# A 16-sequence, four-layer kernel: output product with its operands exchanged, row factors spread by transfers, gates applied on ScalarE, new instruction orders

## The reference, cut to what matters

```python
# B, per head h of 8, expert e of 8; gm is the gate of the chosen expert, else 0
gm = one_hot(argmax(sigmoid(x @ w_gate))) * gates
values = einsum('bhne,ehdk,bnd->bhnk', gm, value_experts, x)
attn = softmax(causal(q * SCALE @ k.T))
out = einsum('bhij,bhjk->bhik', attn, values)
out = einsum('bhne,ehkd,bhnk->bhnd', gm, output_experts, out).sum(heads)
x = layernorm(x + out)
# C: rotation of q and k in pairs of features
rope(x) = stack([x1 * cos - x2 * sin, x2 * cos + x1 * sin])
```

## Time and profile before

| what | value |
|---|---|
| median of 3 runs | 1497.77 us (1497.28 to 1497.99) |
| the profiled execution | 1495.65 us, span of its instructions 1493.8 us |
| TensorE matmul, busy | 1434.7 us, 96% |
| VectorE, busy | 1205.2 us, 81% |
| ScalarE, busy | 820.6 us, 55% |
| GpSimd, busy | 748.6 us, 50% |
| `token_blocks` | from 0 to 1005 us |
| `soft_experts` | from 1005 us to the end |

### The profile page before, as it was taken

One profiled execution on the slowest core, in us unless ns is written; L12 is line 12 of the kernel. 1 busy time (PEld: TensorE's weight loads), 2 busy tenths in 40 slices (PEclk: granted clock), 3 DMA queues, 4 the chain that ended last, 5 costly groups with the idle time before them and its releaser, 6 DMA issues. The chain is left out here.

```text
span 1493.8 us, 32591 instructions
## 1 busy us (share of the span) xinstructions
PE 1434.7 (96%) x10940; PEld 1267.7 (85%) x10940; DVE 1205.2 (81%) x2359; ACT 820.6 (55%) x1850; POOL 748.6 (50%) x1833
## 2 busy tenths in 40 slices
PE   8789999999999999999999999988999999898998
PEld 6658888888888888888888887867999999898998
DVE  6778889889888898898898887768888888757664
ACT  4354555454555464455555544306776777667775
POOL 1433346346355354454453451226777777467772
PEclk8889999999999999999999999998999999999999
DMA  5100000000000000000000004007777777887872
GB/s 194 61 8 8 1 15 2 14 16 1 15 15 2 16 5 12 15 5 12 16 1 15 8 1 128 2 3 174 196 193 193 191 192 195 264 315 297 312 304 75
DMA packets 135426, 130.43 MB, mean 87 GB/s; under 512 B 7232, under 2 KB 125248, under 8 KB 128768
## 3 DMA queue, kind: packets, MB, share of 16 engines
q1 hardware_dynamic: 135296, 128.79, 27.9%
HBM read 72.93 MB, written 55.84 MB: 86 GB/s over the span
## 5 line engine op out<-in xcount | busy, mean ns | idle before, releaser
L737 PE MATMUL ps_l<-ve_f,oe 128*128 128x128 f32 x2048 | 275.7, 279 | 0.8 <-DVE ve_f L1740 0.8
L737 PEld LDWEIGHTS ps_l<-ve_f,oe 128*128 128x128 f32 x2048 | 248.8, 192 | 23.1 <-issue 20.4
L1740 DVE SCALAR_TENSOR_TENSOR ve_f<-ps_s,oT 128x512 f32<-128x512 f32 x248 | 166.7, 681 | 4.1 <-PE ps_l L737 2.3
L2934 POOL TENSOR_TENSOR d_s<-d_ex 128x1024 f32<-128x1024 f32 x31 | 125.2, 4040 | 83.0 <-ACT d_ex L2684 82.8
L1701 DVE COPY_PREDICATED vals<-oh,ps_l 128x1024 f32<-128x1024 int32 x112 | 146.9, 1312 | 19.3 <-PE ps_l L477 17.4
L2559 PE MATMUL ps_s<-d_ex,arena 128*128 128x128 f32 x1024 | 121.1, 277 | 4.6 <-DVE d_ex L2827 4.6
L2559 PEld LDWEIGHTS ps_s<-d_ex,arena 128*128 128x128 f32 x1024 | 118.2, 194 | 5.0 <-DVE d_ex L2827 5.0
L2547 PE MATMUL ps_l<-arena 128*128 (+1 forms) x960 | 114.5, 279 | 3.9 <-ACT d_raw L2679 3.9
L1293 ACT ACTIVATE ve_f<-ps_l,r 128x128 f32<-128x128 f32 x128 | 47.3, 370 | 125.9 <-DVE r L1713 125.6
L2547 PEld LDWEIGHTS ps_l<-arena 128*128 128x128 f32 x960 | 111.9, 195 | 4.1 <-ACT d_raw L2679 4.1
L475 PE MATMUL ps_l<-veH,x1H 128*128 128x512 f32 x256 | 115.2, 450 | 0.1
(11 more groups left out here) (332 smaller groups left out, 3842.7 us busy)
## 6 DMA issues: line engine op xcount, KB each, us to landing
logits<-d_raw SPq DMA_DIRECT2D x128, 256.0 KB, 3.5
e_lt<-logits SPq DMA_DIRECT2D x32, 1024.0 KB, 5.1
y_slots<-d_ys SPq DMA_DIRECT2D x64, 256.0 KB, 4.6
d_ex<-y_slots SPq DMA_DIRECT2D x8, 1024.0 KB, 6.9
e_y<-y_slots SPq DMA_DIRECT2D x6, 1024.0 KB, 7.2
d_w<-W SPq DMA_DIRECT2D x16, 256.0 KB, 3.4
arena<-xT SPq DMA_DIRECT2D x16, 128.0 KB, 2.4
arena<-x SPq DMA_DIRECT2D x16, 128.0 KB, 2.4
```

Source lines behind the costliest of these rows:

```text
L737: last = pe.matmul(ps_u[:, cols], oe[:, hp, e, :], mo[:, n % MO, hp, :], start=False, stop=(e == NE - 1 and hp == HP - 1), skip_group_chec ...
L1740: V.scalar_tensor_tensor(mo[:, n % MO, :, :].rearrange("p a n -> p (a n)"), chosen_of(b, c), float(NE - e), oT[:, u, c, :, :].rearrange("p ...
L2934: G.tensor_tensor(s8[:], part[:, 0:8, :], part[:, 8:16, :], ALU.add).then_inc(n, 1)
```

## The change

1. **Output product.** `b_out` has `mo` as stationary and `oe` as moving operand. The sum comes out with tokens in the partitions, in `ps_m` instead of the second half of `ps_l`. `b_oa` and `b_oat` are gone; `b_res` reads the sum itself. `b_start`, which puts the residual there, has four matmuls of 128 columns instead of two of 256.
2. **Factors by transfers.** `b_rgs`, `b_rgb`, `b_oht`, `b_choice` and the four `b_ot` multiplications are gone. VectorE writes the 16 factors and 16 numbers of each token into `rn`; TensorE turns them once (`b_rnt`, 32x128), ScalarE copies them (`b_rn`), and SP writes 16 KB to DRAM and reads them back into all partitions (`spread`, two transfers of 512 KB into `nb`). ScalarE copies the attention's output (`b_ot`, 2 x 512 columns), one VectorE multiplication of 1024 columns applies the factors (`b_og`), and `b_mo` compares with the numbers in SBUF.
3. **Gate of the values.** `b_vg` is gone; `b_pt` applies the gate as a scale of each row of the turned probabilities, in two activations of 256 and 128 columns instead of one copy of 384.
4. **Scores in two groups.** `b_scores(g)` and `b_pv(g)` take two pairs of heads at once, in both pairs of PSUM banks; `b_rg` runs once.
5. **Rotation.** For the blocks below 13 the pairs are swapped by two transfers from SBUF to SBUF (`swap`); `c_rot` is left for the last three.
6. **Orders.** The orders in `slot`, in the first blocks and in the tail are new on all five engines. `newton`, which computes the roots, is the same in both kernels.

The diff, cut to its core:

```diff
+            def spread(b):
+                sp.wait_ge(q["b_rn"], b + 1)
+                wait(sp, q["b_nb"], 32 * (b - 1))
+                sp.dma_start(rn_dram[b % 2].rearrange("a r n -> (a r) n"), rows_s[0:4 * C * HP, :]
+                             ).then_inc(q["b_rn_out"], 16)
+                sp.wait_ge(q["b_rn_out"], 16 * (b + 1))
+                wait(sp, q["b_mo"], OUTS * b)
+                for a in range(2):
+                    sp.dma_start(nb[DH * a:DH * (a + 1), :, :, :, :].rearrange("p q c h n -> p (q c h n)"),
+                                 rn_dram[b % 2, a:a + 1].rearrange("a r n -> a (r n)").to_broadcast([DH, 2 * C * HP * P])
+                                 ).then_inc(q["b_nb"], 16)
+            def swap(b):
+                sp.wait_ge(q["c_q"], b + 1)
+                wait(sp, q["c_qr"], 2 * b)
+                sp.dma_start(t1[0:P:2, :, :], ql[1:P:2, :, :]).then_inc(q["c_swap"], 16)
+                sp.dma_start(t1[1:P:2, :, :], ql[0:P:2, :, :]).then_inc(q["c_swap"], 16)
...
             for pair in range(2, NB // 2 - 1):
                 for u in range(2):
+                    spread(2 * pair + u - 2)
                     load(2 * pair + u + 1, 1 - u)
+                    swap(2 * pair + u - 3)
                     store(2 * pair + u - 3)
...
+            def b_rnt(b):
+                pe.wait_ge(q["b_rg"], 2 * (b + 1))
+                wait(pe, q["c_x3t"], b - 1)
+                pe.transpose(mixed_home(b)[0:4 * C * HP, 0:P], mixed_of(b), id_f[:]).then_inc(q["b_rn_ps"], 1)
...
+            def b_scores(b, g):
+                if g == 0:
+                    wait(pe, q["b_v"], (NE - 1) * (b + 1))
+                    pe.wait_ge(q["b_qk"], HP * (b + 1))
                 else:
-                    wait(pe, q["b_pt"], HB * b + 2 * hp)
+                    wait(pe, q["b_pt"], HB * b + 4)
...
+            def b_pv(b, g):
+                pe.wait_ge(q["b_pt"], HB * b + 4 * g + 4)
...
-                    last = pe.matmul(ps_u[:, cols], oe[:, hp, e, :], mo[:, n % MO, hp, :], start=False,
+                    last = pe.matmul(sum_of(b)[:, cols], mo[:, n % MO, hp, :], oe[:, hp, e, :], start=False,
                                      stop=(e == NE - 1 and hp == HP - 1), skip_group_check=True)
...
+            def b_ot(b, u, g):
+                act.wait_ge(q["b_pv"], 2 * b + g + 1)
+                wait(act, q["b_mo"], OUTS * (b - 1))
+                copy(oT[:, u, :, 2 * g:2 * g + 2, :].rearrange("p c h n -> p h c n"),
+                     ps_o.rearrange("p (h c n) -> p h c n", h=2, c=C)).then_inc(q["b_ot"], 1)
...
-                copy(pt[:, s, a, :, :].rearrange("p a b -> p (a b)"), ps_v[0][:, a, 0:3 * P]
-                     ).then_inc(q["b_pt"], 1)
+                nc.scalar.activation(pt[:, s, a, 0:2, :].rearrange("p a b -> p (a b)"), ps_v[s][:, a, 0:2 * P], ACT.Copy,
+                                     scale=gx[:, 0, h:h + 1])
+                nc.scalar.activation(pt[:, s, a, 2, :], ps_v[s][:, a, 2 * P:3 * P], ACT.Copy, scale=gx[:, 1, h:h + 1]
+                                     ).then_inc(q["b_pt"], 1)
...
+            def b_og(b, u):
+                dve.wait_ge(q["b_nb"], 32 * (b + 1))
+                dve.wait_ge(q["b_ot"], 2 * (b + 1))
+                V.tensor_tensor(oT[:, u, :, :, :], oT[:, u, :, :, :], nb[:, 0, :, :, :], ALU.mult).then_inc(q["b_og"], 1)
...
             def b_res(b):
-                dve.wait_ge(q["b_oat_ps"], b + 1)
+                dve.wait_ge(q["b_oe"], OUTS * (b + 1))
                 stats(dve, "lnB", b_rows(b), b)
```

More of the change, by code:

```diff
@@ L329, in token_blocks @@
             a_op_ps a_r a_xb a_n a_x1t_ps a_x1h a_x1l a_x1
-            b_g_ps b_eg b_gate b_oht_ps b_oht b_qk_ps b_qk b_v_ps b_v0 b_v b_vg b_s_ps b_max b_p b_pt_ps b_pt
-            b_pv b_rg b_rgs b_rgb_ps b_rgb b_ot b_m_ps b_mo b_oe b_oa b_oat_ps b_x2t_ps b_x2t b_start
-            c_qk_ps c_g c_km c_q c_v_ps c_v c_rot_ps c_qr c_t2 c_krt_ps c_kr c_kv_ps c_kv c_out_ps c_z c_res c_n
+            b_g_ps b_eg b_gate b_qk_ps b_qk b_v_ps b_v0 b_v b_s_ps b_max b_p b_pt_ps b_pt
+            b_pv b_rg b_rn_ps b_rn b_rn_out b_nb b_ot b_og b_mo b_oe b_x2t_ps b_x2t b_start
+            c_qk_ps c_g c_km c_q c_v_ps c_v c_swap c_qr c_t2 c_krt_ps c_kr c_kv_ps c_kv c_out_ps c_z c_res c_n
             c_x3t_ps c_x3t c_x3""".split()
@@ L448, in _ @@
             sp.dma_start(oe[:], o_exp).then_inc(experts_in, 16)
-            for b in range(2, 5):
-                load(b, b % 2)
+            load(2, 0)
+            load(3, 1)
+            spread(0)
+            load(4, 0)
+            spread(1)
+            swap(0)
             store(0)
@@ new lines, in b_start @@
+            def b_start(b, u):
+                if b == 0:
+                    pe.wait_ge(q["b_rn"], 1)
+                wait(pe, norms["lnB"]["rows"], C * b)
+                for c in range(C):
+                    cols = slice(c * P, (c + 1) * P)
+                    pe.matmul(sum_of(b)[:, cols], x1H[:, u, cols], id_r[:], start=(c == 0), stop=False,
+                              skip_group_check=True)
+                    last = pe.matmul(sum_of(b)[:, cols], x1L[:, u, cols], id_r[:], start=False, stop=False,
+                                     skip_group_check=True)
+                last.then_inc(q["b_start"], 1)
@@ L2002, in slot @@
                 if more:
+                    a_conv(t + 1, 0, (2,))
+                    a_conv(t + 1, 0, (3,))
+                if o:
+                    b_mo(t - 2, u, 1, 4)
+                if more:
+                    a_sz(t + 1)
+                    a_conv(t + 1, 1, (1,))
                     a_conv(t + 1, 1, (2,))
-                if c:
-                    c_x3(t - 3)
                 if o:
@@ L2018, in slot @@
                     a_conv(t + 1, 1, (3,))
+                if a:
+                    a_x1l(t, u)
+                if c:
+                    c_x3(t - 3)
+                if b:
+                    b_rg(t - 1)
+                if more:
                     a_xbc(t + 1)
-                if b:
-                    b_ot(t - 1, 1 - u, 3)
             conv_prep()
@@ L2175, in _ @@
             b_mo(Z, 1, 1, 7)
-            c_q(Y)
-            c_v(Y)
-            c_qr(Y)
+            c_ln(Y)
             b_res(Z)
-            c_kv(Y)
             rsqrt(dve, "lnB", Z, 1.0, EPS, norms["lnB"]["moments"], 2 * C, True)
-            c_res(Y, 0)
             b_x2(Z, 1)
+            c_x3(Y)
             c_q(Z)
             c_v(Z)
-            c_ln(Y)
             c_qr(Z)
```

776 lines of the change are left out of this document (290 added, 486 removed).

## The result

| | us |
|---|---|
| kernel before, median of the runs beside it | 1497.5 (1495.5 to 1498.0) |
| kernel after, median of 4 runs | 1510.3 (1507.7 to 1511.1) |
| ratio | 1.0085, 95% interval 1.0067 to 1.0102 |
| forecast | 1508, range 1474 to 1524 |

The kernel after is 0.85% slower. The total is close to the forecast; the places are not, as the stretches show. The page first: busy time of each engine, as in the earlier trace rows.

The account below looks back on a forecast made before the run. TensorE was taken to bound the slots, chains between engines the tail. Slots +10.8, slot 15 -0.4, slot 16 -0.5, first blocks -4, tail +5 gave +10.9 us, forecast 1508 us, range 1474 to 1524.

Parts of the forecast that it names:

- TensorE's work: In each slot: products, turns and rotation removed, less what is added, net -3.2 us.
- The four waits: New TensorE waits per slot, ahead of second scores, second `b_pv`, output products and `c_x3t`: 4.1 us in all.
- Step 4: `a_x1t` to `c_x3t`: 1.52 us to `a_x1l`, then `c_x3` 0.55, against 1.1 of TensorE work: wait 0.85 us.
- The net per slot: Each of 12 slots: work -3.2 plus waits 4.1 gives +0.9 us, +10.8 over the 12.
- The sign that I had named: In the profile of the kernel after, slots would take about 58.4 us.
- the bound for being wrong: The prediction would count as wrong if a slot took under 57 us.
- the rival in which it evens out: Whole kernel: same time within 0.2% (3 us), with slot waits of 3.0 to 3.5 and a tail of +2; chance 0.10.
- The cover of the spread: In a slot: `nb` there 11 to 12 us in, `b_og` placed at 15, 3 us of cover, cost 0.
- The rival "`nb` is late": In slots: the 1 MB read takes 12.4 us, `b_og` holds VectorE, +3.5 us x 12 more, 1550; chance 0.05.
- The tail: After slot 16: Z's first output product and `b_res(Z)` later, a shorter chain behind: +5 us; slot 16 itself -0.5.
- my own bound for being wrong: The prediction would count as wrong if the tail grew by over 10 us.
- The first blocks: Before the 12 slots: small VectorE preparations gone 1.2, scores in two groups 1, slot 2 work 1.8: -4 us.

Follow-up runs that it names:

- run 5: Kernel after with the rotation of all blocks as a product on TensorE again and no swap by transfers: 1518.3 us, ratio 1.0144.
- Runs 1: Kernel after with one output product per slot moved to between the fourth turn and the second scores: 1497.1 us, ratio 1.0011.
- run 2: Kernel after with `a_tz` on ScalarE ahead of the copies of heads 4 to 7: 1489.0 us, ratio 0.9955.
- run 6: Kernel after with one unscaled copy of 384 columns per head, leaving out the gate of the value experts: 1493.2 us, ratio 0.9987.
- run 8: Kernel after with slot reorderings on TensorE, ScalarE and VectorE, `b_mo` spread between convolution steps, and the edits of run 4 and run 7: 1463.7 us, ratio 0.9782.
- run 7: Kernel after with block Z's factors formed, turned and copied earlier in slot 16, the turn in another PSUM bank: 1501.7 us, ratio 1.0043.
- Run 12: A later kernel with slots and tail reordered, plus 20 fill products while TensorE waits for Y's normalization: 1456.5 us, ratio 0.9734.
- run 4: Kernel after with the tail alone changed: `c_ln(Y)` behind `b_res(Z)`, `c_x3t(Y)` behind `c_rot(Z)`, 12 fill products left out: 1504.7 us, ratio 1.0062.
- run 11: Kernel after, unchanged, run and profiled a second time: 1508.5 us, ratio 1.0089.

## Why the prediction was right in the sum and where it was wrong

**TensorE's work: right.** -3.2 us a slot was forecast, -3.38 measured (57.30 to 53.92). The rotation's part was 0.85 by start to next start and 1.0 to 1.09 when put back (run 5).

**The four waits: right in place and releaser, too large in size.** 1.0, 1.45, 0.8 and 0.85 forecast, 4.1 in all; 0.83, 1.30, 0.77 and 0.55 measured, 3.45. Step 4, `a_x1t` to `c_x3t`, was furthest off: 1.82 us from turn to turn instead of the 2.07 that I had added up (1.52 and 0.55). Runs 1, 2, 5, 6 and 8 show that these waits and the work add up to the slot: what was taken away shortened it, by 0.73 for 0.83 in the first.

**The net per slot: wrong, small errors times 12.** +0.9 was forecast, -0.14 measured. It is a difference of two numbers near 3.5: the work was off by 0.18, the waits by 0.65, and I had not taken off the 0.24 us of idle time that the slot before had already. Times 12, that gave +10.8 where -1.7 came. The sign that I had named, slots of about 58.4 us, did not show; the bound for being wrong, under 57, was not reached. For the slots the rival in which it evens out had the truth, with waits of 3.0 to 3.5.

**The cover of the spread: right.** `nb` was forecast 11 to 12 us into the slot with 3 us to spare. The slot from 508.27: the turned rows go out at 511.98, the reads are issued at 513.38, and they take 6.3 us (median), so `nb` is there at 519.7, 11.4 us in; `b_og` starts at 523.10 and waits for nothing. The rival "`nb` is late" has no row in a slot.

**The tail: wrong, and this is where the kernel lost.** +4.5 with slot 16 was forecast, +10.8 measured (+10.2 in the second profile); my own bound for being wrong was 10. From the gates of slot 16, Z's first output product stands at 50.6 us before and 59.7 after, Z's statistics at 68.5 and 81.9, the end at 99.3 and 110.05. So it is +9.1, +4.3 and -2.6 in the three parts, where I had +7.5, +1 and -3.9. The way to the first product was nearly right (968.22, 12 us behind the end of slot 16, for the 10 forecast); run 7 took 3.1 to 3.7 of it back. In the products two things were missed. The first is the clock. The kernel before's ten products in a row run at full clock. In the kernel after the clock falls at 962.9, behind waits of 1.63 us for Y's normalization and 0.47 us for a copy, and is low for 10 us; the wait of 2.21 us for the late `b_mo` comes only after that. The first two calls take 3.79 us instead of 1.95:

```profile
956.00:962.90 6.90, 4.24 (x32) 3.61 (x31) 1.40 (x6) 1.68 (x4) 2.73 (x14) 1.00 0.44 95
962.90:973.20 10.30, 7.81 (x29) 6.42 (x28) 5.96 (x8) 1.57 (x4) 1.79 (x3) 0.50 0.19 41
```

```profile
968.22 3.79 PE L748 MATMUL ps_s<-oe,ve_f 128*128 128x128 f32 x16 [2.21 <-DVE ve_f L1649]
```

Run 12 shows full clock to be worth 3.8 us in the version where it was tried. The second is VectorE's order at the end: with `c_ln(Y)` ahead of `b_res(Z)` the statistics came 2.1 us late, as run 4 shows. I had counted the missing `c_ln(Y)` behind the statistics as a gain of 1.5 and its cost ahead of them not at all. These parts were measured in different versions and don't have to add up in one; why the last part gave 2.6 and not 3.9 was not followed.

**The first blocks: wrong.** "Scores in two groups save part of the chain", -1, with -4 in all. +5.5 came in the profile, of which 2.6 are the clock's up to 60 us (run 11). For the rest, the kernel before and run 4, which has the kernel after's first blocks and started them at nearly the same time and clock. The stretches go from block 0's first query product to its first scores, to its first output product, to the gates of slot 3. Before:

```profile
60.49:80.81 20.32, 19.31 (x98) 16.74 (x98) 16.30 (x22) 6.24 (x14) 4.54 (x9) 0.87 0.00 1
80.81:129.43 48.62, 43.55 (x258) 31.97 (x259) 37.79 (x81) 23.65 (x72) 15.94 (x45) 0.89 0.02 6
129.43:160.76 31.33, 31.09 (x265) 26.70 (x264) 24.81 (x61) 17.13 (x56) 9.28 (x43) 1.00 0.04 10
```

Run 4:

```profile
60.35:82.84 22.49, 21.70 (x111) 18.78 (x111) 18.30 (x25) 6.10 (x13) 6.01 (x16) 0.88 0.00 1
82.84:130.54 47.70, 38.71 (x224) 29.07 (x225) 32.05 (x66) 22.80 (x71) 11.24 (x35) 0.89 0.12 29
130.54:163.03 32.49, 30.38 (x259) 26.47 (x259) 24.56 (x58) 16.73 (x60) 13.67 (x48) 1.00 0.03 10
```

TensorE has 3.2 us less to do and is idle 5.6 us more. The first scores come 2.2 us later: in both pairs of PSUM banks, they stand behind the last value products, which use the same banks. Behind them TensorE has 4.8 us less to do and gets 0.9 of it: with little to fill in, the chain of scores, maxima, exponentials and copies leaves it idle 9.0 us instead of 5.1. In slot 2 the waits of the later slots are there already, 2.1 us instead of 0.2. In block 0 of the kernel after the second scores wait 1.59 us for the last copy, where the earlier trace rows has 0.26. That grouping and order are the cause was read from these rows and not tried.

**So** the forecast's total came right by luck: an error of 12.5 us in the slots (measured below forecast) met one of 9.5 in the first blocks and one of 6.3 in the tail, both the other way. 2.6 of the 9.5 are the clock's spread, which nobody could forecast from one profile. What was forecast as the cause, waits that take back what TensorE was relieved of, is real and was shown; it made the change worth nothing in the slots. What made the kernel slower stands outside them.
